# Summing gathered rows as high and low halves in the first half of layer 0

## The reference

```python
h = jnp.maximum(_layernorm(x, axis=-1), 0.0)
x = x + _L0_gnn_ref(h, edge_index, L0_gnn_W1, L0_gnn_b1, L0_gnn_W2, L0_gnn_b2)

def gnn_layer(x, W, b, src, dst):          # called twice: W1, b1 and then W2, b2
    h = x @ W.T + b
    msgs = h[src]
    agg = jax.ops.segment_sum(msgs, dst, num_segments=N_NODES)
    return jax.nn.relu(agg)
```

## Time and profile before

| what | value |
|---|---|
| median of 3 timed runs | 3077.48 us (3076.08 to 3077.89) |
| the profiled execution's own time | 3067.87 us |
| its span in the trace | 3065.9 us |
| TensorE busy | 2706.2 us (88%), 14594 records |
| VectorE busy | 2012.9 us (66%) |
| ScalarE busy | 1231.6 us (40%) |
| GpSimd busy | 1833.0 us (60%) |
| sums of the a_ stage, first and last | 446.7 and 757.3 us from the span's start |

### The profile page before, as it was taken

How to read it: one execution, slowest core, us unless ns; L and a number is a source line. 1 busy time by engine, 2 the same in 40 slices (tenths; PEclk the granted TensorE clock), 3 DMA queues, 4 the chain that set the end, 5 groups by cost and what they waited for, 6 DMA issues and landing times. The chain is left out here.

```text
span 3065.9 us, 53080 instructions
## 1 busy us (share of the span) xinstructions
PE 2706.2 (88%) x14594; PEld 2271.0 (74%) x14594; DVE 2012.9 (66%) x5558; ACT 1231.6 (40%) x2621; POOL 1833.0 (60%) x2162
## 2 busy tenths in 40 slices
PE   1279829999799996999999969999999599999998
PEld 1146518888677775999999958888888488888886
DVE  6867646665465653766666648999999555555555
ACT  0057615444455553444444424333333243333332
POOL 4657726554577775766666637776767445555553
PEclk9999999999899998999999989999999799999999
DMA  9982043333444543333333314433333244444443
GB/s 273 322 246 65 2 145 95 105 117 103 116 138 144 153 153 111 119 104 104 104 104 104 104 63 122 123 112 111 111 115 112 81 131 139 139 139 138 139 139 104
DMA packets 144688, 386.98 MB, mean 126 GB/s; under 512 B 32795, under 2 KB 33755, under 8 KB 144002
## 3 DMA queue, kind: packets, MB, share of 16 engines
q0 software_dynamic: 101408, 304.38, 33.4%
q1 hardware_dynamic: 42130, 79.44, 8.2%
q10 hardware_dynamic: 1056, 2.10, 0.2%
HBM read 261.22 MB, written 149.28 MB: 134 GB/s over the span
## 5 line engine op out<-in xcount | busy, mean ns | idle before, releaser
L1916 DVE SCALAR_TENSOR_TENSOR f_Mlo<-f_pm,f_Mhi 128x512 fp32r<-128x512 f32 x80 | 55.3, 692 | 263.6 <-ACT f_Mhi L1883 263.6
L803 POOL DMA_INDIRECT f_Gsrc<-rows,indexS x80 | 77.1, 964 | 217.8 <-PE f_phsrc L1955 211.9
L1883 ACT ACTIVATE f_Mhi<-f_pm 128x512 fp32r<-128x512 f32 x80 | 47.8, 598 | 376.4 <-PE f_pm L785 376.4
L1480 PE MATMUL c_pu<-c_Zhi,parts 128*128 128x256 f32 x640 | 183.2, 286 | 4.4 <-DVE c_Zlo L1403 4.4
L1482 PE MATMUL c_pu<-c_Zhi,parts 128*128 128x256 f32 x640 | 182.2, 285 | 0.0
L1649 ACT CAST d_Thi<-d_pt 128x512 fp32r<-128x512 f32 x80 | 46.9, 587 | 334.1 <-DVE d_pt L776 334.1
L1481 PE MATMUL c_pu<-c_Zlo,parts 128*128 128x256 f32 x640 | 180.6, 282 | 0.0
L1368 ACT ACTIVATE c_pu<-c_pu,c_b1col 128x256 f32<-128x256 f32 x160 | 61.8, 448 | 278.1 <-PE c_pu L1482 278.1
L807 POOL DMA_INDIRECT h<-a_rows,indexD x80 | 80.5, 1007 | 122.6 <-ACT a_rows L1061 117.8
L1469 PE MATMUL c_pt<-c_sel,c_G 128*128 128x128 f32 x640 | 124.7, 277 | 24.2 <-ACT c_H L1355 24.2
L783 PE MATMUL a_po<-parts,a_Thi 128*128 128x512 f32 x320 | 132.5, 414 | 3.5 <-DVE a_Tlo L1093 3.4
(11 more groups left out here) (458 smaller groups left out, 10045.2 us busy)
## 6 DMA issues: line engine op xcount, KB each, us to landing
rows<-n_xt SPq DMA_DIRECT2D x80, 260.0 KB, 4.0
n_xt<-in_x SPq DMA_DIRECT2D x80, 256.0 KB, 4.0
h<-q_zerorow SPq DMA_DIRECT2D x80, 256.0 KB
selrowsD<-selD SPq DMA_DIRECT2D x1, 2640.0 KB, 9.3
selrowsS<-selS SPq DMA_DIRECT2D x1, 2640.0 KB, 14.7
q_keyrowD<-in_dst POOLq DMA_DIRECT2D x1, 2560.0 KB
q_keyrowS<-in_src POOLq DMA_DIRECT2D x1, 2560.0 KB, 30.8
o_wstage<-in_L_W ACTq DMA_DIRECT2D x2, 1024.0 KB, 6.2
```

The lines of the kernel that those rows point to most:

```text
L803: return pool.indirect_dma_start(out, None, table, bass.IndirectOffsetOnAxis(ap=rows, axis=0))
L1480: pe.matmul(psum_u[:, o, :], g.Whi[2][:, c, cols], Zhi[:, c, :], start=c == 0, stop=False)
L1916: dve.scalar_tensor_tensor(Mlo[s][:, :], psum_m[s][:, :], 0.0, Mhi[s][:, :].bitcast(F32), ALU.max, ALU.subtract).then_inc(s_Mlo, 1)
```

## The change

G, as normalised by ScalarE, is copied by ScalarE to `Ghi` in float32r (new `high_row`), and VectorE subtracts the copy from G and writes the rest to `Glo` in float32r (new `low_row`). `sel`, which holds ones and zeros, becomes float32r. The sum over a chunk of 128 features is then two float32r matmuls that add up in PSUM, with Ghi's and Glo's columns as weights, in place of one in fp32. The sum now waits for `s_Glo` in place of `s_Gn`. Ghi and Glo have two buffers each; both new steps wait until the sum two tiles earlier is done. The second half of layer 0 (`second`) uses the same code with its old branches.

```diff
         G = e.ring("G", U, [P, D if second else EXT], F32)
-        sel = e.ring("sel", 2, [P, P], F32)
+        sel = e.ring("sel", 2, [P, P], F32 if second else F32R)
+        if not second:
+            Ghi, Glo = e.ring("Ghi", 2, [P, D], F32R), e.ring("Glo", 2, [P, D], F32R)
+            s_Ghi, s_Glo = e.sem("s_Ghi"), e.sem("s_Glo")
...
+            def high_row(T):
+                act.wait_ge(s_Gn, T.t + 1)
+                wait(act, s_summed, T.t - 1)
+                nc.scalar.copy(Ghi[T.slot(2)][:, :], G[T.slot(U)][:, 0:D]).then_inc(s_Ghi, 1)
...
                     else:
+                        at(i, u, 2, U, NT, high_row)
                         at(i, u, 3, U, NT, norm_in)
...
+            def low_row(T):
+                s = T.slot(2)
+                dve.wait_ge(s_Ghi, T.t + 1)
+                wait(dve, s_summed, T.t - 1)
+                dve.tensor_tensor(Glo[s][:, :], G[T.slot(U)][:, 0:D], Ghi[s][:, :].bitcast(F32), ALU.subtract)\
+                    .then_inc(s_Glo, 1)
...
                     at(i, u, 1, U, NT, low_sum)
+                    if not second:
+                        at(i, u, 2, U, NT, low_row)
...
                 else:
-                    pe.wait_ge(s_Gn, T.t + 1)
+                    pe.wait_ge(s_Glo, T.t + 1)
                 wait(pe, s_Tlo, T.t - 1)
                 for c in range(C):
-                    ins = pe.matmul(psum_t[s][:, c, :], G[T.slot(U)][:, c * P:(c + 1) * P], sel[s][:, :],
-                                    start=True, stop=True)
+                    cols = slice(c * P, (c + 1) * P)
+                    if second:
+                        ins = pe.matmul(psum_t[s][:, c, :], G[T.slot(U)][:, cols], sel[s][:, :], start=True, stop=True)
+                    else:
+                        pe.matmul(psum_t[s][:, c, :], Ghi[s][:, cols], sel[s][:, :], start=True, stop=False)
+                        ins = pe.matmul(psum_t[s][:, c, :], Glo[s][:, cols], sel[s][:, :], start=False, stop=True)
                 ins.then_inc(s_summed, 1)
```

## The result

| | before | after |
|---|---|---|
| median of 5 timed runs each, us | 3077.48 (3075.69 to 3079.76) | 3092.43 (3087.78 to 3094.55) |
| ratio, 95% interval | | 1.0048 (1.0037 to 1.0059) |
| the profiled execution's own time | 3067.87 | 3092.43 |
| from tile 0's norm_in to tile 0's first product | 4.80 | 8.50 |
| from tile 0's norm_in to its node list | 8.39 | 13.72 |

The changed kernel is slower by 15 us, 0.5%. The profiled executions differ by 24.6, so they mislead if they are compared whole: 7.8 of it lie ahead of the stage, in unchanged code (tile 0's norm_in starts at 445.72 in one and 453.50 in the other), and 4.3 behind it, where the code is the same as well. I therefore measure all runs by the stage, from the first norm_in on. It grew by 12.2 us: 5.3 up to the first node list, 6.9 at the two splits, nothing in the other tiles.

The account below looks back on a forecast made before the run. TensorE was taken as the bound of layer 0's first half. Terms +2.6, +4.3 and +3.2 gave +10.1 us on 3067.87, so 3078.0, or 3087.6 as a median; predicted 3087.5, range 3053 to 3098, the forecast's own 3081 to 3094.

Parts of the forecast that it names:

- The pace of a record: Sum's 8 TensorE matmul records a tile: 0.116 us each against fp32's 0.112, +2.6 us over 80 tiles.
- The high end of 0.120: Upper pace in us for a sum record, taken from three records of 256 moving columns in 0.36 us.
- The rival at 0.0655: Sum on TensorE: weight loads hide behind 128-column matmuls, records take 0.0655 us, period 3.50, total 3056 us; chance 0.27.
- The no-gain rival at 0.224: Sum on TensorE: float32r gains nothing over fp32 at 128 columns, 0.224 us a record, total 3155 us; chance 0.07.
- high_row and low_row in a steady tile: ScalarE copy and VectorE subtraction in steady tiles: both hidden by the products of the tile before, 0 us.
- The new-wait rival: GpSimd's indirect transfer holds VectorE's low_row, each tile loses 0.3 us: +23 more, total 3110 us; chance 0.08.
- The start: First tiles of the stage: later first products and some at the lower clock, +4.3 us, range 2.9 to 5.8.
- The two splits: GpSimd's weight splits: the next sum waits behind low_row, +1.6 us each, +3.2 in all, range 1.5 to 5.
- From the profiled execution to the median: Whole kernel: the median lay 9.6 us above the profiled execution, so 3078.0 becomes 3087.6.

Follow-up runs that it names:

- The runs with another order: Changed kernel with high_row ahead of relu and low_row behind the bias (3085.87 us), behind carried (3082.68), or behind carried with bf16 halves (3056.39).
- the run with the high half alone: Changed kernel without low_row and the low half's matmuls, four float32r matmuls a tile: 3048.25 us, ratio 0.9903 against the kernel before.
- the fp32 sum: Changed kernel keeping high_row, low_row and the new waits, but summing in fp32 from G: 3093.06 us, ratio 1.0044 against the kernel before.
- both steps early: Changed kernel with high_row ahead of relu on ScalarE and low_row right behind the bias on VectorE: 3085.87 us, ratio 1.0027 against the kernel before.

## Why the prediction was right, and where not

**Sign and size.** Forecast +10.1 us on the stage and 3087.6; measured +12.2 on the stage and 3092.4. The mechanism was the one described: no gain in the steady part, a longer start, a longer stall at the splits. That the sum is off by 2.1 us only is in part luck: start and splits together were put 4.7 too low, and the 2.6 for a slower record, which did not come, made up for half of it.

**The pace of a record.** Taken as 0.116, measured 0.112: +2.6 us became 0. The argument from the difference of the loads' widths held, and the experiments with 96 columns and with bf16 made it a measured one. The high end of 0.120 came from 256 moving columns. By the line through 256 and 512 these take 0.109, not the 0.107 of the prediction, which is as long as the load; which of the two sets the 0.120 there is not shown. The ends of this term, by its own paces of 0.109 and 0.120, are −1.9 and +5.1, not −1 and +6. The rival at 0.0655 needed loads that hide behind 128 moving columns. They do in bf16 and do not in float32r. The no-gain rival at 0.224 is excluded.

The Trainium skill, "TensorE: Matmul & The Clock Gate", section "Back-to-back issue gap", measured about 81 ns for a matmul of 128 columns in a stream of loads and matmuls. This shape ran at 112 in float32r and fp32 and at 55 in bf16; 81 was met in neither.

**high_row and low_row in a steady tile.** Costed at nothing, and so it is. low_row was placed 604.48 − 601.62 = 2.86 us behind the start of a sum; it starts 604.99 − 602.14 = 2.85 behind. The copy took 0.62, as the cast of the earlier trace rows. The new-wait rival falls: the indirect transfer did not hold low_row.

**What the split holds.** The step held in the earlier trace rows reads one tensor, in SBUF, so it does not by itself show that low_row, which reads two, can be held. The runs with another order do, with 4.66 and 4.55 us.

**The start.** +4.3, in 2.9 to 5.8; measured +5.3. The first product came 3.7 later (forecast 2.9 to 3.8). The rest is the lower clock: I priced four products at it, and it was all 12, 1.6 us.

**The two splits.** This is the term that was mis-sized: +3.2 forecast with 1.5 to 5, +6.9 measured. The step was "0.7 for that and 0.9 for the sum, which used to run inside the stall, come after it". That part was near: the wait went from 1.7 on the mean to 3.6, +1.9 each. What the step left out is that the longer wait also costs the clock: 0.50 granted behind it, where the earlier trace rows's waits of up to 1.8 had kept 1.00 (a wait of 1.67 lost it in the run with the high half alone, so that may have been chance). It makes up the other 1.5 to 1.6 each. The same thing is in the start, and there I had seen the pace of 0.43 in the earlier trace rows; I didn't ask whether a stall of 3.6 could bring it back.

**From the profiled execution to the median.** The forecast added 9.6 to the execution's own time. That was needed: the stage accounts for 12.2 of the 15 between the medians. The other 3 are no more than the noise: the interval of the ratio is 11.4 to 18.2 us.

What stays open: what decides when the clock falls, and for how long. With equal waits the first split lost more than the second in several runs, and the difference is the time at 0.50. With the fp32 sum the wait was 3.65 us twice, the clock was low for 6.8 us and for 3.4, and the tiles took 10.58 and 9.34. With both steps early the wait was 2.12 twice, the clock was low for 3.4 us and not at all, and the tiles took 8.50 and 6.91. And whether a split placed elsewhere, or on another engine, would cost nothing was not tried. In the run with the high half alone one split cost nothing at its own place, where steps of VectorE with an operand in PSUM came first.

## What to carry to other kernels

Where 128-column weights in float32r meet 128 moving columns, the load set TensorE's pace here, and fp32's records had the same pace. Going from fp32 to two float32r halves keeps both the number of loads and their length and buys nothing; bf16 halves take half the time a record, where their bits do. Before a step is put ahead of the bottleneck engine, look for the one place where a queue in front of it is already held by something else: there it costs its own time, the work that used to run inside the stall, and perhaps the clock behind it. It also matters which of VectorE's steps stands there: those with an operand in PSUM were not held.

## What the runs showed of the hardware

- A float32r record of 128 x 128 takes 0.112 us, as each of fp32's two; 0.086 with 96 weight columns, unchanged with 96 moving ones. At the start, where the products stand 0.43 apart and not 0.23, the same records stand 0.21 apart. So the load slows down with the clock too:

```profile
456.08 0.41 PE L1216 MATMUL a_pt<-a_sel,a_Glo 128*128 128x128 f32 x1
456.29 0.41 PE L1215 MATMUL a_pt<-a_sel,a_Ghi 128*128 128x128 f32 x1
```

- The granted-clock column can't be trusted where the trace has no reading of the clock. At the start of the changed stage it reads 1.00 while the products go 0.43 apart; the trace's readings begin at 467.2, just where TensorE's pace doubles, and the column shows 1.00 for all that lies ahead of them, even with TensorE idle:

```profile
462.00:467.00 5.00, 5.00 (x13) 3.94 (x14) 2.26 (x7) 1.82 (x3) 0.94 (x1) 1.00 0.20 53
```

13 records in 5 us is the pace of 1.2 GHz. The distance between starts is the better witness there.

- Inside the busy part of the stage, over all runs, every wait of TensorE of 3.56 us or more (ten) came with a granted clock of 0.50, for 3.4 us and twice for 6.8. Shorter waits did not decide it: 1.60, 1.84, 1.92, 2.12, 2.87, 3.04 and 3.16 us kept 1.00, while 1.67, 1.93, 2.12, 2.30, 2.53, 2.54, 2.86, 2.99 and 3.25 lost it.
- A gather that shares GpSimd's queue with the split comes late, and the step that waits for it holds its whole engine: norm_in waited 6.52 us, and TensorE 4.11 behind it.
- GpSimd's subtraction holds the first VectorE step whose operands all lie in SBUF: list_nodes of 0.26 took 4.58, low_row of 0.69 took 4.66. Steps with an operand in PSUM kept their times inside it: low_sum 0.69, the bias 0.75, carried 0.22. Cut in four, it held such SBUF steps by one piece each; they took 1.10 to 1.38 us.
